# Nine instead of six aided rows per group, and a last group that begins eight steps later, in a four-layer graph network on one core

## The reference

```python
xh = (h @ W).reshape(n, H, C)
alpha = leaky_relu(a_src[src] + a_dst[dst], 0.2)        # one score per edge and head
alpha = exp(alpha - segment_max(alpha, dst)[dst])
denom = segment_sum(alpha, dst)
out = segment_sum(xh[src] * alpha[:, :, None], dst) / denom
```

## Time and profile before

| | |
|---|---|
| median of 3 runs | 4219.95 us (4216.05 to 4226.9) |
| the profiled execution, its own time | 4214.28 us |
| its span | 4212.5 us, granted TensorE clock 0.843 |
| PE busy | 2836.2 us (67%) |
| DVE busy | 3092.9 us (73%) |
| ACT busy | 2403.7 us (57%) |
| POOL busy | 2666.3 us (63%) |
| DMA packets | 127620, 298.57 MB |

### The profile page before, as it was taken

How to read it: one execution, slowest core, us unless ns; L and a number is a source line. 1 busy time by engine, 2 the same in 40 slices (tenths; PEclk the granted TensorE clock), 3 DMA queues, 4 the chain that set the end, 5 groups by cost and what they waited for, 6 DMA issues and landing times. The chain is left out here.

```text
span 4212.5 us, 58543 instructions
## 1 busy us (share of the span) xinstructions
PE 2836.2 (67%) x16208; PEld 1802.9 (43%) x16208; DVE 3092.9 (73%) x9684; ACT 2403.7 (57%) x5241; POOL 2666.3 (63%) x2801
## 2 busy tenths in 40 slices
PE   1899998974576766764546767676635676766763
PEld 1344445543354544543334535444423354544542
DVE  6999994564576776778667877777855676776785
ACT  1888882005566666662646656666365566666644
POOL 5766660305777777773577777777347777777743
PEclk8999999986788888987678888889857888888886
DMA  3111112632222222221232223323112222222210
GB/s 104 56 83 83 59 80 96 227 134 61 64 69 69 68 69 69 65 69 29 52 71 70 66 70 70 71 70 71 27 40 64 69 69 68 68 69 68 66 48 16
DMA packets 127620, 298.57 MB, mean 71 GB/s; under 512 B 45412, under 2 KB 74972, under 8 KB 123712
## 3 DMA queue, kind: packets, MB, share of 16 engines
q0 software_dynamic: 74976, 155.58, 16.3%
q1 hardware_dynamic: 52320, 139.24, 9.8%
HBM read 241.28 MB, written 53.38 MB: 70 GB/s over the span
## 5 line engine op out<-in xcount | busy, mean ns | idle before, releaser
L1416 POOL DMA_INDIRECT work<-table,lane_src x2184 | 2092.5, 958 | 665.3 <-issue 644.6
L1513 PE MATMUL psum<-work 128*128 128x396 bf16 (+1 forms) x5850 | 1162.9, 354 | 67.1 <-ACT work L1458 32.1
L1455 ACT ACTIVATE work<-work,middle_node_number 128x384 f16<-128x384 f16 x1587 | 954.4, 601 | 225.2 <-PE psum L1513 205.0
L1458 ACT ACTIVATE work<-work 128x384 bf16<-128x384 f16 x1587 | 829.7, 523 | 50.5
L1570 PE MATMUL psum<-work 128*128 128x136 f32 x4836 | 701.4, 303 | 186.2 <-DVE work L1701 95.2
L1513 PEld LDWEIGHTS psum<-work 128*128 128x128 bf16 x5850 | 597.5, 104 | 511.6 <-issue 122.3
L1570 PEld LDWEIGHTS psum<-work 128*128 128x128 f32 x4836 | 653.5, 208 | 272.2 <-issue 159.1
L1738 DVE TENSOR_TENSOR node_sums<-node_sums,psum 128x136 f32 x2418 | 558.0, 292 | 105.2 <-PE psum L1570 98.1
L793 POOL TENSOR_SCALAR work<-work 128x128 f16<-128x128 f16 x392 | 335.5, 857 | 220.3 <-PE psum L808 193.0
L771 DVE TENSOR_SCALAR work<-work 128x400 f16<-128x400 f16 x1568 | 461.2, 316 | 1.4 <-PE psum L808 0.8
L741 PE MATMUL psum<-work 128*128 128x448 f16 x2100 | 451.4, 352 | 3.2 <-PEq L1166 2.5
(11 more groups left out here) (374 smaller groups left out, 2927.5 us busy)
## 6 DMA issues: line engine op xcount, KB each, us to landing
counts<-work SPq DMA_DIRECT2D x14, 2800.0 KB, 8.3
work<-counts SPq DMA_DIRECT2D x14, 2800.0 KB, 9.8
work<-table,lane_src POOLq DMA_INDIRECT x2184, 2.5
work<-spread SPq DMA_DIRECT2D x78, 256.0 KB, 4.0
work<-masks SPq DMA_DIRECT2D x78, 128.0 KB, 3.0
work<-source_rows SPq DMA_DIRECT2D x39, 192.0 KB, 3.7
spread<-node_sums SPq DMA_DIRECT2D x4, 896.0 KB, 9.0
table<-work SPq DMA_DIRECT2D x10, 330.0 KB, 3.0
```

Source lines behind the costliest of these rows:

```text
L1416: pool.indirect_dma_start(m.ring[:, s % SLOTS, 0:F + H], None, m.d_table[H], bass.IndirectOffsetOnAxis(ap=m.src[:, s:s + 1], axis=0)).then ...
L1455: act.activation(away, rows_of(g, u), ACT.Abs, bias=m.low_tile[:, hi:hi + 1]).then_inc(far_known, 1)
L1458: act.activation(hot_of(g, u), away, ACT.Relu, bias=1.0, scale=-1.0).then_inc(hot_act, 1)
L1513: mm = pe.matmul(aid_banks[:, k, 0:3 * (F + H)], hot_of(g, u)[:, k * P:(k + 1) * P], m.all_thirds[:, :, hi, 0:F + H], start=(hi == 0), sto ...
```

## The change

```diff
-LAST_LO = (GROUPS - 1) * GROUP - 8
+LAST_LO = (GROUPS - 1) * GROUP
...
-AIDED = 6
+AIDED = 9
 HOTS = 12
 CHAIN_HOTS = (6, 2, 4)
-PART_HOTS = (3, 3, 3, 4, 4, 4, 4, 4)
-PART_DVE = (1, 1, 1, 1, 1, 1, 1, 1)
-GAP_HOTS = (6, 3)
-TAKEN_IN = (4,)
+PART_HOTS = (4, 4, 5, 8, 8, 9, 4, 4)
+PART_DVE = (2, 2, 2, 3, 3, 3, 2, 2)
+GAP_HOTS = (9, 8)
+TAKEN_IN = (3, 6)
```

## The result

| | before | after |
|---|---|---|
| median of 4 runs | 4218.0 us | 4357.36 us (4354.86 to 4358.2) |
| ratio | | 1.0329, 95% interval 1.0314 to 1.0345 |
| span of the profiled execution | 4212.5 us | 4355.6 us |
| granted TensorE clock | 0.843 | 0.885 |

What follows compares the result with a forecast made beforehand. POOL's gather queue was taken to bound the kernel before, and ACT to end full periods after. Layers of +29.5 us twice and +47.1, together +106 on 4214.3, gave 4320 us, range 4200 to 4370.

Steps and rivals of the forecast that it cites:

- the chain: PE, DVE and ACT in a full period: block 7 at 53.9, unit 66 at 56.3, ACT last, period 74.2 us.
- the queue that was reckoned: ACT, at most 12 units ahead of PE, waits for buffers some 6.7 us a period and is done at 72.3.
- PE's wide parts: PE from block 1's products to the end of block 5's units: five products and 34 units, ending at 48.2 us.
- DVE has message, one-hot, 2 or 3 units and the adding: DVE's work beside PE's 34 units: 4.5 to 4.8 us a block and one take, so PE is the slower.
- The clock term: Score stage: less low clock lets its first six units gain 0.2 us, period 74.4 to 74.2.
- Eight heads: DVE's extra work, mostly in the score stage, adds 2.9 us a period, giving 77.1; bounds 0 and 3.2.
- starts and last groups: Per layer: first score stage needs 3 gathers fewer, -3.8 us; last group has one block less, -4.0 us.
- The split: Full periods lose 1.4 us each; groups 10 and 11 much more, their 63.0 and 59.2 us periods becoming full ones.
- The gathers stay the bound: Rival: POOL's gathers still set the periods, 68.9 us or 70.3 with eight heads; 4117 us, faster; chance 0.09.
- ACT waits less: Rival: ACT held only by PE's first wide part, periods 71.7 us or 74.6 with eight heads; 4234 us; chance 0.16.
- The clock falls more often: Rival: low clock at PE's waits at 50 and 53 or reaching block 1's units, +1.5 us a period; 4374; chance 0.10.
- The clock stays full: Rival: no low clock at the score stage's start or block 0, periods 70.1 or 73.0 us; 4173, faster; chance 0.07.

Runs made afterwards that it cites:

- e3: The changed kernel with 14 one-hot buffers instead of 12: 4242.7 us, 1.0059 of the kernel before.
- e4: The changed kernel with DVE making all four units of blocks 6 and 7, ACT 52 units instead of 56: 4360.0 us, 1.0339 of the kernel before.
- e5: The changed kernel with DVE making four more units, 69 to 72, while it waits for PE's turn of the spread: 4244.1 us, 1.007 of the kernel before.
- e1: The kernel before with only the last group's later start (LAST_LO = 768), still six aided rows: 4242.5 us, 1.0065 of the kernel before.
- e9: e6 and e8 together: 4134.3 us, 0.9808 of the kernel before.
- e6: e3 and e5 together, plus units laid evenly behind the blocks and two units before block 0: 4144.2 us, 0.9833 of the kernel before.
- e13: e9 with four units instead of two before block 0, two fewer ahead of the drop's matmuls: 4146.0 us, 0.9835 of the kernel before.
- e8: e5 with DVE's two one-hots ahead of the third take and the columns of blocks 0 and 1 copied last: 4234.5 us, 1.0047 of the kernel before.
- e12: The changed kernel with two units moved from ahead of the drop's matmuls to before block 0: 4340.1 us, 1.0303 of the kernel before.

## Why the prediction was right, and where it was off

**The direction and the mechanism** were right. POOL ceased to be the bound (87.1 us of slot waits), and the chain came where it was put: block 7's products at 54.7 us in the period (forecast 53.9), unit 66 at 57.3 (56.3), ACT done at 73.3 (72.3), the next stage at 75.1 (74.2). ACT's waits are those of the queue that was reckoned: 6.8 us in this period, forecast 6.7. The prediction says in one place that POOL's waits for slots hardly change and in another that they would be a sign; they rose from 20.7 to 87.1 us, and the second is right. e3, e4 and e5 show the mechanism: buffers, and units behind the last wait, matter, and units ahead of it do not.

**A term too small** is the time of PE's wide parts, forecast to end at 48.2. They end at 48.9. About half of that is PE's wait for the first take, 0.65 us where 0.3 was reckoned. The step that failed besides is "DVE has message, one-hot, 2 or 3 units and the adding": DVE's three units in block 5 must themselves wait for a buffer (0.46 us), and 0.51 of issue, which the profile doesn't explain, lies behind them; so the adding of block 4 comes late and PE's block 5 waits 0.23. I had applied the limit of 12 to ACT alone. In e3, with 14 buffers, DVE's wait there and PE's wait at block 5 are gone, and PE's wait for the first take is 0.28.

**The clock term**, 0.2 us gained, came to nothing. I let the first low stretch shrink to the 3.4 us of the earlier trace rows. In the changed kernel it is 6.8 us in most periods with four heads, 3.7 of it before the stage and 3.2 in it, and 3.2 is what the period at 1443.61 that I reckoned from had; its messages start at 13.2, those of the changed kernel at 13.3. The two low stretches of the changed kernel, the first from the stage's start on:

```profile
1449.90:1453.10 3.20, 3.20 (x12) 1.47 (x10) 2.85 (x8) 3.10 (x7) 2.53 (x3) 0.50 0.27 62
1463.30:1470.10 6.80, 5.66 (x22) 4.63 (x23) 6.14 (x15) 6.50 (x13) 5.05 (x6) 0.50 0.56 134
```

The two terms together are 0.9 a period. **Eight heads**: I took 2.9 us over the other layers, and it was 3.2, the bound I had given. The periods' sum is thus 34 us over the forecast's, and starts and last groups gave 20.2 instead of 23.4: 37 us, from 106 to 143. The measured 4357 lies just above what the forecast gave itself with a period 1 us either way (4284 to 4356): each error is small, and all are of one sign.

**The split** the prediction pointed at was right: full periods lose 2.2 us with four heads and 4.1 with eight, and groups 10 and 11 lose 12 to 14 each. e1 shows that the group boundary alone costs 26 us with six rows.

**The rivals.** The gathers stay the bound: not in this kernel, but in e9 with four heads, so the floor was the right one. ACT waits less: the waits are as reckoned. The clock falls more often: its 4374 is nearer to the measured time than the forecast is, but not by its mechanism. In none of the 36 periods is the clock low at 50 or 53 us, and the second stretch ends before block 1's products begin (20.2 and 21.3 us with four heads, 22.5 and 23.8 at the latest with eight). The clock stays full: rows 6 spoke against it, and both stretches are there. It names, though, what e6 later gained by. The rule quoted from the Trainium skill, "TensorE: Matmul & The Clock Gate", Part 1 (The HAM clock gate), that activity releases the throttle, agrees with e6 (granted clock 1.00 around block 0, where PE has more to do in the stage). e13, with as many units in the stage, has low clock in every period, so by these runs their place counts too.

Two of the rivals' sums are a few us off by their own terms: ACT waits less comes to 4238 (not 4234), and the clock stays full to 4179 (not 4173). Neither changes a conclusion.

## What to carry to other kernels

Idle time on an engine isn't room for work that must pass in order through others. Before moving work off the bounding queue, write down for one period which wait ends last on each engine once that queue is faster, with every ring of buffers as a limit on all its producers, and put the new work where the engines wait now. When a wait for a buffer ends a period, more buffers, or units taken off behind the last such wait, are worth more than less work ahead of it.

## What the runs showed of the hardware that was not expected

- The clock and the period hang together, though not in one direction. In e5, with periods between 70.7 and 72.4 us in the first attention layer, those without a low stretch at the start have messages at 11.6 us, and those where it lasts to 4.8 or 5.0 at 14.0. PE's idle time before the stage is 14.8 us in the kernel before, 5.7 in the changed one and 3.2 in e5, and the low stretch becomes shorter with it. But in e8, with 2.3 us of idle time, it begins later and reaches to 3.3 us or so into the stage, and the messages come 0.5 later than in e5.
- Two units of three matmuls, about 1 us of PE's work, taken from behind blocks 0 and 1 into the score stage, took the low stretch around block 0 (granted clock 0.51, then 1.00) from 22 of 36 periods and 72 us from the time, 1.7%; most of what PE gains is the clock, by the comparison under e6. The same amount of work only moved within the stage (e12, e13) left it in all periods.
- A gather costs POOL no more beside 795 one-hots of DVE than beside 363: 957 ns (958 before), and in the median 1.249 us from one start to the next, in both kernels and in all three layers.
